# Windowed attention: the residual as one fused VectorE operation, the join with the rows above on VectorE, another order of transfers

## What is computed

```python
y = _gn(x)                                    # group norm
crop = y[windows of 16 x 16 at a step of 14]  # 19 x 19 windows a batch
tok = crop as (windows, 256, 96)
q, k, v = layernorm(tok) @ wq, @ wk, @ wv     # 4 heads
out = softmax(q k' / 4) v @ wproj + tok
acc = zeros; acc[windows] += out              # overlapping rows and columns meet
x2 = acc * fh * fw                            # halves where windows overlap
... MLP with a 5 x 5 depthwise convolution on x2 ...
x = x + layer(y)
```

## Time and profile before

| | us |
|---|---|
| median of 3 runs | 7102.86 (7101.3 to 7104.74) |
| profiled execution | 7065.86 |
| its span | 7064.1 |
| PE busy | 6050.0 (86%) |
| DVE busy | 4893.7 (69%) |
| ACT busy | 3489.9 (49%) |
| POOL busy | 3103.3 (44%) |

### The profile page before, as it was taken

How to read it: one execution, slowest core, us unless ns; L and a number is a source line. 1 busy time by engine, 2 the same in 40 slices (tenths; PEclk the granted TensorE clock), 3 DMA queues, 4 the chain that set the end, 5 groups by cost and what they waited for, 6 DMA issues and landing times. The chain is left out here.

```text
span 7064.1 us, 136670 instructions
## 1 busy us (share of the span) xinstructions
PE 6050.0 (86%) x51768; PEld 3121.7 (44%) x51768; DVE 4893.7 (69%) x7120; ACT 3489.9 (49%) x5182; POOL 3103.3 (44%) x4987
## 2 busy tenths in 40 slices
PE   0885999999999999999999589989997766588885
PEld 0332555555555555555555233335554111076661
DVE  7796777777777777777777355558886545556664
ACT  0553666666666666666666356644443111154340
POOL 0443677777776777777776656610000000000000
PEclk9997999999999999999999799999999888799995
DMA  7685344444444444444443598788897999636665
GB/s 306 195 242 162 72 99 105 102 102 105 105 105 95 101 101 99 99 103 99 99 95 71 129 273 238 233 289 343 345 345 261 297 306 309 205 103 201 190 187 180
DMA packets 761672, 1252.70 MB, mean 177 GB/s; under 512 B 159364, under 2 KB 477828, under 8 KB 730948
## 3 DMA queue, kind: packets, MB, share of 16 engines
q1 hardware_dynamic: 700532, 1090.77, 55.3%
q10 hardware_dynamic: 53328, 102.85, 4.9%
q0 software_dynamic: 7168, 50.34, 2.1%
HBM read 680.81 MB, written 508.40 MB: 168 GB/s over the span
## 5 line engine op out<-in xcount | busy, mean ns | idle before, releaser
L816 DVE TENSOR_REDUCE at_mz<-at_ps 128x4 bf16<-128x1024 f32 x1444 | 1771.2, 1227 | 557.5 <-PE at_ps L735 550.1
L683 ACT ACTIVATE at_E<-at_ps 128x1024 f32<-128x1024 f32 x1444 | 1399.4, 1021 | 387.0 <-PE at_ps L747 368.6
L747 PE MATMUL at_ps<-at_qaug,at_k 32*128 32x256 f32 x11552 | 847.0, 408 | 26.6 <-DVE at_qaug L843 26.6
L758 PE MATMUL at_ps<-at_E,at_vaug 128*32 128x256 f32 x11552 | 782.5, 388 | 5.3
L1282 PE MATMUL cv_ps<-cv_yin,cv_band 128*128 128x384 f32 x2304 | 746.4, 486 | 26.2 <-DMA cv_yin<-y_mlp 26.2
L747 PEld LDWEIGHTS at_ps<-at_qaug,at_k 32*128 32x128 f32 x11552 | 532.1, 188 | 509.8 <-issue 350.1
L1302 DVE TENSOR_TENSOR cv_yin<-cv_gl,cv_yin 64x384 f32<-64x384 f32 x1152 | 637.4, 553 | 150.4 <-ACT cv_gl L1293 142.6
L1564 POOL MEMSET cs_eps<- 96x1 f32 x1 | 0.1, 95 | 1500.5 <-POOLq L1312 1500.5
L735 PE MATMUL at_ps<-at_k,at_q 32*128 32x256 bf16 x5776 | 578.0, 276 | 9.0 <-DMA at_k<-at_packed 7.5
L1282 PEld LDWEIGHTS cv_ps<-cv_yin,cv_band 128*128 128x128 f32 x2304 | 436.7, 190 | 336.2 <-DMA cv_yin<-y_mlp 27.1
L1293 ACT ACTIVATE cv_gl<-cv_ps,cv_bias 128x384 f32<-128x384 f32 x576 | 334.4, 581 | 437.4 <-PE cv_ps L1282 437.4
(11 more groups left out here) (217 smaller groups left out, 10351.0 us busy)
## 6 DMA issues: line engine op xcount, KB each, us to landing
cv_yin<-y_mlp SPq DMA_DIRECT2D x48, 2340.0 KB, 14.8
s_mlp<-cv_yin SPq DMA_DIRECT2D x48, 2340.0 KB, 8.4
at_rows_in<-y_attention SPq DMA_DIRECT2D x76, 768.0 KB, 6.2
gn_xin<-in_x SPq DMA_DIRECT2D x16, 3072.0 KB, 23.2
ln_xin<-in_x SPq DMA_DIRECT2D x192, 256.0 KB, 7.3
y_attention<-ln_xin SPq DMA_DIRECT2D x192, 256.0 KB, 3.8
cl_xu<-x SPq DMA_DIRECT2D x128, 384.0 KB, 3.7
cl_xv<-x SPq DMA_DIRECT2D x64, 768.0 KB, 6.3
```

Of the source, the lines that this page charges most:

```text
L683: act.activation(E[:, m % 2, 2 * p:2 * p + 2, :], psum[:, 2 + 2 * p:4 + 2 * p, :], ACT.Exp).then_inc(exp_done, 1)
L747: i = pe.matmul(psum[:, 2 + h, TOK * j:TOK * j + TOK], k[rows, n % 2, tokens(w, 128 * j, 128)], qaug[rows, m % 2, :], start=True, stop=True)
L758: i = pe.matmul(pv_ps[32 * h:32 * h + VC, 0:TOK], vaug[:, m % 2, z, h, :], E[:, m % 2, h, z * TOK:(z + 1) * TOK], start=(z == 0), stop=(z ...
L816: dve.tensor_reduce(mz[:, m % 2].rearrange("p j (h c) -> p h j c", c=32)[:, 2 * p:2 * p + 2, :, DQ], psum[:, 0:2, :].rearrange("p h (j n) ...
```

## The change

`turn_back` leaves its places in the running band and goes to slots 0 to 7 of the next band, ahead of the second reduce; the join follows it at once on DVE. `saved` gets a second buffer, and `save` runs one slot ahead. The projections move to slots 1 to 8, queries and keys to 9 to 16, the second half of the turned columns to slots 6 to 9. The residual becomes one `scalar_tensor_tensor` on DVE in slots 9 to 16 (after the last band in slots 2 to 9), and `both` moves to 10 to 17. `xscaled` goes. SP's order changes: the first half of the y after next goes ahead of the spreads, the store of x2 behind them. The loop has one slot more.

```diff
-    QK_AT = 8
-    END = NW + YP
+    PROJ_AT, QK_AT, RES_AT, BOTH_AT = 1, 9, 9, 10
+    END = NW + PROJ_AT + YP
...
-        saved = sb("saved", [128, CC, STEP])
-        xscaled = sb("xscaled", [C, PS, CC])
+        saved = sb("saved", [128, 2, CC, STEP])
...
+        def back_at(n):
             nb, w = where(n)
             return (nb - 1, w) if 1 <= nb <= NB and w < YP else None
+        def proj_at(n):
+            nb, w = where(n)
+            return (nb - 1, w - PROJ_AT) if 1 <= nb <= NB and PROJ_AT <= w < PROJ_AT + YP else None
+        def residual_at(n):
+            nb, w = where(n)
+            first = RES_AT if nb < NB else PROJ_AT + 1
+            return (nb - 1, w - first) if 1 <= nb <= NB and first <= w < first + YP else None
...
                     load_y(n + 1, 1)
-                if n:
-                    store_x2(n - 1)
+                if n + 2 < NB:
+                    load_y(n + 2, 0)
                 if more:
                     spread_heads(n + 1, 0)
                     spread_heads(n + 1, 1)
                 if n:
                     store_xs(n - 1, 0)
-                if n + 2 < NB:
-                    load_y(n + 2, 0)
...
                     spread_heads(n + 1, 3)
                 if n:
+                    store_x2(n - 1)
                     store_xs(n - 1, 1)
...
-            def join(n, c):
-                rows = shared_rows(n)
-                if rows:
-                    pool.wait_ge(ot_done, YP * n + c + 1)
-                    pool.wait_ge(saved_done, joins(n, c))
-                    a = ot[:, cols(c), 0:rows]
-                    pool.tensor_tensor(a, a, saved[:, :, 0:rows], ALU.add).then_inc(joined, 1)
-            def residual(n, c):
-                rows = own_rows(n)
...
-                pool.tensor_scalar(xscaled[:, 0:rows, :], xr[:, 0:rows, cols(c)], t["gn_scale"][:, n // NWIN:n // NWIN + 1], None, ALU.mult).then_inc(scaled, 1)
...
-                pool.tensor_tensor(a, a, xscaled[:, 0:rows, :], ALU.add).then_inc(x2_done, 1)
...
-            for n in range(END + 1):
+            for n in range(END):
                 nb, w = where(n)
-                if whole(n - 5):
-                    join(*whole(n - 5))
+                if back_at(n + 1):
+                    save(*back_at(n + 1))
                 if 0 <= n - 3 < NW:
                     normalise(n - 3)
-                if whole(n - 3):
-                    save(*whole(n - 3))
                 if nb + 1 < NB and w < 4:
                     turn_columns(nb + 1, w)
-                if nb + 1 < NB and 9 <= w < 13:
-                    turn_columns(nb + 1, w - 5)
-                if nb >= 1 and 1 <= w < 1 + YP:
-                    residual(nb - 1, w - 1)
-                if nb >= 1 and nb < NB and 9 <= w < 9 + YP:
-                    both(nb - 1, w - 9)
+                if nb + 1 < NB and 6 <= w < 10:
+                    turn_columns(nb + 1, w - 2)
+                if both_at(n):
+                    both(*both_at(n))
...
             def turn_back(n, c):
...
                 dve.transpose(ot[:, cols(c), :].rearrange("p c r -> p (c r)"),
                               heads[:, 16 * c:16 * c + 16, :].rearrange("p a d -> p (a d)")).then_inc(ot_done, 1)
+                if rows:
+                    dve.wait_ge(ot_done, YP * n + c + 1)
+                    a = ot[:, cols(c), 0:rows]
+                    dve.tensor_tensor(a, a, saved[:, c % 2, :, 0:rows], ALU.add).then_inc(joined, 1)
+            def residual(n, c):
+                rows = own_rows(n)
+                dve.wait_ge(pr_out, YP * n + c + 1)
+                if c % 4 == 0:
+                    dve.wait_ge(x_loaded[c // 4], 16 * (n + 1))
+                a = xa[:, 0:rows, cols(c)]
+                dve.scalar_tensor_tensor(out=a, in0=xr[:, 0:rows, cols(c)], scalar=t["gn_scale"][:, n // NWIN:n // NWIN + 1], in1=a,
+                                         op0=ALU.mult, op1=ALU.add).then_inc(x2_done, 1)
...
-            for n in range(NW + 4):
+            for n in range(END + 1):
                 if n < NW:
                     maxima(n, 0)
                 if 0 <= n - 3 < NW:
                     turn(n - 3)
+                if back_at(n):
+                    turn_back(*back_at(n))
+                if residual_at(n):
+                    residual(*residual_at(n))
                 if n < NW:
                     maxima(n, 1)
                 if 0 <= n - 3 < NW:
                     denominators(n - 3)
-                if whole(n - 4):
-                    turn_back(*whole(n - 4))
```

More of the change, by code:

```diff
@@ L419, in attention @@
             sem(s) for s in ("max_done", "qaug_done", "turned_done", "rden_done", "ot_done"))
-        share_done, weighted, heads_done, saved_done, joined, scaled = (
-            sem(s) for s in ("share_done", "weighted", "heads_done", "saved_done", "joined", "scaled"))
+        share_done, weighted, heads_done, saved_done, joined = (
+            sem(s) for s in ("share_done", "weighted", "heads_done", "saved_done", "joined"))
         x_loaded = [sem(f"x_loaded{i}") for i in range(2)]
@@ L469, in qk_at, with both_at @@
             return (nb + 1, w - QK_AT) if n < NW and nb + 1 < NB and QK_AT <= w < QK_AT + YP else None
-        def whole(n):
+        def back_at(n):
             nb, w = where(n)
-            return (nb, WHOLE_AT.index(w)) if 0 <= n < NW and w in WHOLE_AT else None
+            return (nb - 1, w) if 1 <= nb <= NB and w < YP else None
         def proj_at(n):
             nb, w = where(n)
-            return (nb - 1, w) if 1 <= nb <= NB and w < YP else None
+            return (nb - 1, w - PROJ_AT) if 1 <= nb <= NB and PROJ_AT <= w < PROJ_AT + YP else None
[3 more added lines that the diff above has]
+            return (nb - 1, w - first) if 1 <= nb <= NB and first <= w < first + YP else None
+        def both_at(n):
+            nb, w = where(n)
+            return (nb - 1, w - BOTH_AT) if 1 <= nb < NB and BOTH_AT <= w < BOTH_AT + YP else None
         @block.sync
@@ L606, in save @@
                 if rows:
-                    if n % NWIN == 1:
+                    if shared_rows(n - 1):
+                        pool.wait_ge(joined, joins(n - 1, c))
+                    else:
                         pool.wait_ge(ot_done, YP * (n - 1) + c + 1)
[L609 to L613, removed]
-            def join(n, c):
-                rows = shared_rows(n)
-                if rows:
-                    pool.wait_ge(ot_done, YP * n + c + 1)
-                    pool.wait_ge(saved_done, joins(n, c))
-                    a = ot[:, cols(c), 0:rows]
-                    pool.tensor_tensor(a, a, saved[:, :, 0:rows], ALU.add).then_inc(joined, 1)
-            def residual(n, c):
-                rows = own_rows(n)
[L625 to L628, removed]
-                pool.tensor_scalar(xscaled[:, 0:rows, :], xr[:, 0:rows, cols(c)], t["gn_scale"][:, n // NWIN:n // NWIN + 1], None, ALU.mult).then_inc(scaled, 1)
-                pool.wait_ge(pr_out, YP * n + c + 1)
-                pool.wait_ge(scaled, YP * n + c + 1)
-                a = xa[:, 0:rows, cols(c)]
-                pool.tensor_tensor(a, a, xscaled[:, 0:rows, :], ALU.add).then_inc(x2_done, 1)
+                    if joins(n, c) > 2:
+                        pool.wait_ge(joined, joins(n, c) - 2)
+                    pool.tensor_copy(saved[:, c % 2, :, 0:rows], ot[:, cols(c), PS - rows:PS]).then_inc(saved_done, 1)
             def both(n, c):
@@ L829, in turn_back @@
             def turn_back(n, c):
+                rows = shared_rows(n)
                 dve.wait_ge(heads_done, NWIN * n + WHOLE_AT[c] + 1)
-                if shared_rows(n):
+                if rows:
                     dve.wait_ge(saved_done, joins(n, c))
```

## The result

| | before | after |
|---|---|---|
| runs of this comparison: median (lowest to highest), us | 7102.08 (7089.81 to 7104.74) | 6996.3 (6975.82 to 7003.67) |
| ratio after / before, 95% interval | | 0.985 [0.9824, 0.9875] |
| profiled execution (span), us | 7065.9 (7064.1) | 6989.15 (6987.4) |
| busy: PE, DVE, ACT, POOL, us | 6050.0, 4893.7, 3489.9, 3103.3 | 6017.8, 5212.7, 3497.1, 2290.2 |

The change makes the kernel 106 us faster; the forecast said 74 (7029, range 6990 to 7095). The page after: engines, and PE's busy tenths in 40 slices.

A forecast was written before the change was run, and what follows sets the result against it. PE was taken to pace the attention slots, with a DMA stall of 97 us on top. Terms -97 + 5 + 18 + 4 + 3 - 7 = -74 us gave 7029 us, range 6990 to 7095.

The forecast's parts named there:

- What bounds the kernel, and where the 100 us were: Attention stage: PE sets the slot pace; 100 us lost beyond the summed slots, nearly all where ACT's copy awaits spreads.
- The stall, -97: ACT's copy of queries and keys waits for spreads behind the x2 store; reordering transfers removes the whole stall, -97 us.
- turn_back and join on DVE, +5, +18 and +4: DVE's added work: +5 us in projection slots, +18 in slot 0, +4 for the first batch's last band.
- the bound of 0.35 by POOL's join: Upper bound for DVE's join, from the same join on POOL: 0.35 us would add +38 us; 0.22 was taken.
- The residual, +3: Key slots 9 to 16: fused residual takes 0.63 us after waiting 0.39 for POOL's addition, +0.01 a slot, +3 us.
- The tail, -7: After the last window: residuals on DVE beside POOL's additions give -11 us, later projections +4, together -7.
- The offset of 37 us: Whole kernel: profiled execution 37 us below the runs' median; the same offset carried 6992 to the forecast 7029.
- The thought that the offset was more stall: Forecast's range: 30 us more gain if the runs' extra 37 us over the profile are stalls too.
- the first, a part of the stall stays: Load of y fills the queue, first pair lands 3 us later, half the stall stays: 7077 us; chance 0.13.
- The second, the late store: x2 store lands 2 us late, holding up ACT's first projection of the next band: 7103 us, no change; chance 0.10.
- The third, a residual held up for nearly the whole of a POOL operation: Slots 9 to 16: POOL's lock makes DVE the bound, +207 us, 7236 (7139 if work alone takes 1.0); chance 0.15.

The follow-up runs named there:

- run 2: Kernel before with only the store of x2 moved behind the second pair's spread: 6998.19 us, ratio 0.9863 to the kernel before.
- run 1: The kernel before, unedited, profiled once more: 7110.07 us, reach of the reduces 3230.2 us.
- Run 6: The changed kernel with each join's addition made twice on DVE, the first into a spare tile: 7028.8 us, ratio 0.9913 to the kernel before.
- runs 7 and 9: Kernel before with x2's store behind the second spread and the fused residual on DVE in slots 4 to 11, measured twice: 6976.84 and 6979.87 us.
- run 4: Kernel before with only the residual moved to DVE, fused, in slots 1 to 8, old transfer order: 6989.93 us, ratio 0.9852.
- run 5: The changed kernel with the load of y put back behind the store of xs: 7115.47 us, ratio 1.0032 to the kernel before.
- run 3: Kernel before with only the store of x2 moved behind the last spread: 7024.87 us, ratio 0.9906.

## Why the prediction was right, point by point

**What bounds the kernel, and where the 100 us were:** right. Taking the x2 store from ahead of the spreads (run 2) gives the gain, the copy's waits end with it, and the bands come out at the 82.4 us that the slots summed to.

**The stall, -97:** right in its mechanism, short in its size. The reach fell by 84.6 us against the earlier trace rows although DVE's work adds 18 (below), so 103 us went; against run 1's reach it is 112. The slots say the same: slots 12 and 13 took 11.85 us before in the mean of 36 bands (12.12 in run 1) and 9.04 in run 2, which makes 101 (111). So 6 to 15 of the 32 us by which the medians' fall, 106, passes the forecast's 74 are here. The first pair landed 9.0 us after its first issue (9.7 forecast, 10.8 before), and the fifth copy came 3.3 us behind that landing, where 2.1 were reckoned. That PE works at its lower clock after such a wait was left out of the mechanism. The 97 held it all the same, since it was a difference between the trace and the sum of slots; the prices of the rivals did not. From the second band on the granted clock was 0.985 before and 1.00 in the change.

**turn_back and join on DVE, +5, +18 and +4:** the duration was met (0.23 for 0.22, the second reduce at 2.35 for 2.34), and the bound of 0.35 by POOL's join was far off. From the second reduce to the next slot, however, DVE takes 1.95, not the 2.04 that the prediction made with a row of a plain slot. So its slot is 4.29 and not 4.38: slot 0 costs 0.39 instead of 0.49, and the projection slots, where PE's 4.35 is longer, nothing instead of 5 us. Run 6 shows the edge. Net of small gains in other slots a steady band is 0.28 longer than in run 2, 9.5 us in 34 bands. The sum took slots 1 to 7 of every band for projection slots. In bands 18 and 37, behind a band with two rows of its own to project, all eight are plain ones: 3.90 in run 2 and 4.29 in the change, 3.1 us more in each of the two bands, which the prediction does not have. Band 19, with the joins of 14 rows, is 2.6 us longer, of 4 predicted. That makes 18 us in all. The version of runs 7 and 9, without these costs, has a reach 14 and 16 us shorter, or 17.6 and 17.3 with the first bands taken out.

**The residual, +3:** nothing. Its work was sized well, 0.63 for the 0.64 of a free one. The step that failed is that this work was put wholly behind POOL's end: only 0.48 us of it come behind, so a residual that meets POOL takes 0.88 instead of 1.02 and ends 0.15 sooner, and red1 keeps its 2.41. That it meets POOL near the end of an operation, by 0.4 us, is as predicted. The Trainium skill ("SBUF — State Buffer", Who interferes with whom) has the two exclude each other for a whole instruction; the traces agree but for the residual's first 0.16 of 0.64 us: its end comes 0.48 us behind POOL's in the change and in run 4 alike.

**The tail, -7:** from the last reduce to the first row of the next stage it is 42.1 us where it was 49.7: -7.6. Run 4, with the residual alone on DVE, has 42.0, so the residual earns it. That the sum fits is luck, though. POOL's last addition ends 31.9 us behind the last reduce in the change, 28.6 in run 4 and 44.6 before: -16 from the residual's move where -11 was reckoned, and +3.3 from the later projections (+4). The last store then takes 9.7 us to land in the change and 12.8 in run 4, right behind the other two, where it took 4.5; this term was not in the sum. These last rows of POOL in the stage after the change answer to the earlier trace rows:

```profile
3848.42 2.91 POOL L628 TENSOR_TENSOR at_xr<-at_xr,at_xa 96x512 f32<-96x512 f32 x2
3851.96 1.25 POOL L628 TENSOR_TENSOR at_xr<-at_xr,at_xa 96x512 f32<-96x512 f32 x1 [0.63 <-DVE at_xa L834]
3854.99 1.25 POOL L628 TENSOR_TENSOR at_xr<-at_xr,at_xa 96x512 f32<-96x512 f32 x1 [1.77 <-DVE at_xa L834]
```

The last additions now run beside DVE's residuals and wait for them; one is left at the end instead of eight.

**The step that was mis-sized:** the costs. 30 us were charged (5 + 18 + 4 + 3) and 18 paid, and the stall was 6 to 15 us larger. Both lean the same way, by 18 to 27 of the 32 us; the rest is no more than runs of one kernel differ by. In the profiles the stage, first reduce to the next stage's first row, went from 3270.2 (run 1: 3279.9) to 3178.1, by 92 to 102 us. The two profiled executions differ by 77 us, close to the 74, but by luck: what comes before the stage took 6 us more in the second one and what comes behind it 10. The offset of 37 us was carried over in full; the kernel after was profiled only 7 us below its median. The thought that the offset was more stall was wrong for the most part: of the 44 us between run 1 and the first profile 31 lie in later stages.

**The rivals:** the first, a part of the stall stays, is refuted in the change (one wait, 10 us), though run 5 shows how near another one is: with the load of y at the other place, the other end of the band starves. The second, the late store, is a true mechanism (run 3) that the change avoids by some 2.5 us. The third, a residual held up for nearly the whole of a POOL operation, happened nowhere in the change's steady bands, where all 272 residuals of 448 elements are booked 0.80 to 0.89; run 4 has it once a band, 0.75 of the copy's 1.06.

## What to carry to other kernels

When a wait for a DMA recurs once per block, look at what stands ahead of that transfer in its queue and at what that in turn waits for: a store that waits for late arithmetic holds back every load behind it. Moving the arithmetic or moving the store may each be the cure, so try the one that costs no engine time alone before crediting a bundle; and when a step is moved later, its store and the loads around it have to be placed again, since in this change one load's place decided between 1.5% faster and 0.3% slower. Work put into an engine's idle time is free up to the slot's other bound and costs in full from there, so compute both chains, each with rows of its own kind of slot, and count the blocks at the edges, whose slots are of another kind.

## What was not expected of the hardware

- A wait of 2.57 us cost PE 1.45 us more behind it, at a granted clock of 0.60 over 4 us (run 5). Over the stage, 56 us more of idle PE came with 60 us more of busy PE for the same products. From the kernel before to the one after, PE's time in the stage fell by 57 us idle and 35 busy.
- The hold-up between POOL and DVE works both ways. In run 4 a join on POOL, 0.35 us by itself, took 0.74 where DVE's residual was under way, and the residual 1.23 where POOL's copy was.
- The fused operation on two SBUF operands of 448 elements takes 0.64 us where no POOL operation runs beside it (run 4), in line with the 0.55 of 384 elements in the earlier trace rows. Where it meets one it ends 0.48 us behind it, whether 0.40 or 0.75 us went by before. turn_back (one SBUF operand) took 0.67 in the change as in the earlier trace rows.
